# First attention's head loop: GpSimd negates the query factor, both state sums stand ahead of its power, three quantization passes move to slot 5, one C broadcast moves behind the attention products

## The reference, cut to what matters

```python
# layer 0, cross attention: 16 heads of 128, 4 batches of 256 queries and 256 keys
q = rmsnorm((hidden_states @ Wq).reshape(B, Sq, H, D), gq)
k = rmsnorm((encoder_hidden_states @ Wk).reshape(B, Skv, H, D), gk)
scores = einsum('bqhd,bkhd->bhqk', q, k) * scale
out = einsum('bhqk,bkhd->bqhd', softmax(scores), v) ... @ Wo
# layer 0, feed-forward: weights rounded in blocks of 32 to a tiny float format
q = round(x / scale) * scale, clipped to max_norm      # _q_w(w_gate), _q_w(w_up), _q_w(w_down)
# layer 3, state space block: 16 states, scanned over 256 steps for 4 batches and 256 channels
state = state * dA + (d * u)[..., None] * b[:, None, :]
y = einsum('bdn,bn->bd', state, c)                      # y is a sum over the 16 states
```

## Time and profile before

| | |
|---|---|
| median of 3 runs (lowest, highest) | 1078.1 us (1078.09, 1079.49) |
| profiled execution: its time, its span | 1078.1 us, 1076.6 us |
| PE busy | 878.0 us, 82% of the span |
| DVE busy | 764.5 us, 71% |
| ACT busy | 490.1 us, 46% |
| POOL busy | 332.1 us, 31% |

### The profile page before, as it was taken

The page is one execution under the profiler, slowest core; times in us unless marked ns, Lnnn a source line. Parts: engine busy times, 40 slices in busy tenths (PEclk is TensorE's granted clock), DMA queues, the critical chain, the costliest instruction groups (busy, mean ns, idle before and its releaser), DMA issues.

```text
span 1076.6 us, 12899 instructions
## 1 busy us (share of the span) xinstructions
PE 878.0 (82%) x4348; PEld 620.3 (58%) x4352; DVE 764.5 (71%) x1505; ACT 490.1 (46%) x855; POOL 332.1 (31%) x210
## 2 busy tenths in 40 slices
PE   5786988898989888865658988667687889999998
PEld 3355776666767666643335464454576776545656
DVE  5248799999998989889973856856889874353311
ACT  2484665565656555633321334443576664111111
POOL 2012244433333343425471000203465740510000
PEclk8899999999999999886677999885789999999999
DMA  3012000000000000000502000000000000300000
GB/s 120 16 40 93 16 15 15 24 20 15 15 15 15 15 17 1 5 0 1 190 0 79 1 0 1 1 1 1 1 1 2 1 1 1 125 0 1 10 10 20
DMA packets 12924, 24.25 MB, mean 23 GB/s; under 512 B 4280, under 2 KB 8656, under 8 KB 11728
## 3 DMA queue, kind: packets, MB, share of 16 engines
q1 hardware_dynamic: 12448, 20.53, 5.7%
q10 hardware_dynamic: 432, 3.15, 0.7%
HBM read 22.63 MB, written 1.05 MB: 22 GB/s over the span
## 4 chain that ended last, share of the span: by engine, by line
PE 29%; DVE 16%; issue 5%; ACT 4%; POOL 1%; ACTq 0%; DVEq 0%
PE PS L2088 12%; PE PS L2137 6%; PE PS L2191 3%; DVE mxf L1541 2%; DVE regD L1579 1%; PE PS L1992 1%; PE PS L1641 1%; PE PS L1968 1%; DVE regB L1579 1%; DVE regA L1291 1%; DVE mx_am L1242 1%; PE PS L2155 1%; PE PS L2006 1%; PE PS L2175 1%; PE PS L2176 1%
## 5 line engine op out<-in xcount | busy, mean ns | idle before, releaser
L476 POOL TENSOR_TENSOR y<-y,regB 128x1024 f32<-128x1024 f32 x32 | 76.3, 2389 | 162.7 <-DVE regB L1096 162.7
L450 POOL TENSOR_SCALAR veps<-mv 128x4 f32<-128x4 f32 x16 | 7.4, 463 | 273.7 <-DVE mv L977 273.7
L679 ACT ACTIVATE regA<-PS,nb,rq 128x256 f32<-128x256 f32 x128 | 71.4, 566 | 32.9 <-DVE regA L1057 31.7
L1057 DVE TENSOR_SCALAR_CACHE_REDUCE regA<-PS,nrq 128x256 bf16<-128x256 f32 x128 | 55.8, 473 | 31.7 <-PE PS L1716 30.0
L1747 PE MATMUL PS<-regA 128*128 128x256 f32 x256 | 69.6, 396 | 9.9 <-DVE X L1070 9.9
L2191 PE MATMUL PS<-regA 128*128 128x128 f32 x512 | 74.8, 294 | 3.4 <-ACT regA L931 3.3
L1085 DVE TENSOR_TENSOR_SCAN regB<-regB 128x1024 f32<-128x1024 f32 x32 | 72.8, 2279 | 0.1
L2191 PEld LDWEIGHTS PS<-regA 128*128 128x128 f32 x512 | 68.2, 207 | 7.1 <-ACT regA L931 6.0
L1738 PE MATMUL PS<-regA 128*128 128x256 f32 x256 | 67.4, 386 | 5.7 <-DVE qss L1044 5.6
L1716 PE MATMUL PS<-regA 128*128 128x256 f32 x256 | 66.8, 384 | 0.0
L1070 DVE SCALAR_TENSOR_TENSOR X<-PS,ls,X 128x256 f32<-128x256 f32 x128 | 55.4, 475 | 14.2 <-PE PS L1747 13.5
(11 more groups left out here) (270 smaller groups left out, 2140.9 us busy)
## 6 DMA issues: line engine op xcount, KB each, us to landing
regA<-in_W SPq DMA_DIRECT2D x16, 384.0 KB, 3.0
regB<-in_wg SPq DMA_DIRECT2D x2, 1024.0 KB, 6.5
regB<-in_wu SPq DMA_DIRECT2D x2, 1024.0 KB, 8.4
X<-in_x SPq DMA_DIRECT2D x1, 1024.0 KB, 7.6
regC<-in_wg ACTq DMA_DIRECT2D x1, 1024.0 KB, 4.7
regC<-in_wu ACTq DMA_DIRECT2D x1, 1024.0 KB, 7.4
regC<-in_wd ACTq DMA_DIRECT2D x1, 1024.0 KB, 10.4
regB<-in_wd SPq DMA_DIRECT2D x1, 1024.0 KB, 9.0
```

The source lines that it names most:

```text
L476: pool.tensor_tensor(halves(y3, i), halves(y3, i), halves(prod, i), ALU.add).then_inc(y_done, 1)
L679: act.activation(p0[i][:, q, :], bank(S_BANK + i)[:, q * S:(q + 1) * S], ACT.Exp, bias=nb0[:, i, q:q + 1], scale=rq[par][:, 2 * b + q:2 * ...
L1057: ins = dve.tensor_scalar(spill[:, i, q, :], bank(S_BANK + i)[:, q * S:(q + 1) * S], nrq[par][:, t:t + 1], None, ALU.mult, ALU.min, accum_ ...
```

## The change

Four edits, all in this loop. POOL computes `nrq` itself, with a product of `rq` and a tile of -1 right behind the power, and DVE only waits for it. On POOL the second y sum of a head goes ahead of the query power, behind the key power. DVE does its three quantization passes L1141 to L1143 at the end of slot 5 instead of slot 6. PE issues the broadcast of the second half of C (index 3) behind `heads` and `output` of slot b = 2 instead of ahead of them.

```diff
+        negone = sb("negone", [P, NT])
...
+            pool.memset(negone[:, :], -1.0).then_inc(const_set, 1)
...
-            pool.wait_ge(const_set, 4)
+            pool.wait_ge(const_set, 5)
...
             def query_scale(h, par):
                 pool.wait_ge(qss_done, h + 1)
                 pool.tensor_tensor(rq[par][:, :], qss[:, :], neghalf[:, 0:NT], ALU.pow).then_inc(rq_done, 1)
+                pool.wait_ge(rq_done, h + 1)
+                pool.tensor_tensor(nrq[par][:, :], rq[par][:, :], negone[:, :], ALU.mult).then_inc(nrq_done, 1)
...
                     scan_sum(n, 0)
                     key_scale(hp * 2 + (par + 1))
+                    scan_sum(n, 1)
                     query_scale(hp * 2 + (par + 1), 1 - par)
-                    scan_sum(n, 1)
                     (block_values if par else block_units)(hp)
...
-            def query_factor(h, par):
-                dve.wait_ge(rq_done, h + 1)
-                link(dve.tensor_scalar(nrq[par][:, :], rq[par][:, :], -1.0, None, ALU.mult))
...
-                elif s == 6:
+                elif s == 5:
                     dve.wait_ge(mxu_done, hp)
                     link(dve.tensor_scalar(mx_c.bitcast(I32), part.bitcast(I32), EXPO, None, ALU.bitwise_and))
                     link(dve.tensor_scalar(mx_c, mx_c, 1.0, 1.5 * 2.0 ** 22, ALU.max, ALU.mult))
                     link(dve.tensor_scalar(part, part, 6.0, -6.0, ALU.min, ALU.max))
...
-                            query_factor(h, par)
+                            dve.wait_ge(nrq_done, h + 1)
...
                         elif b == 2:
-                            broadcast_state(n, 3) if more else broadcast_state(n + 1, 1)
+                            if not more:
+                                broadcast_state(n + 1, 1)
...
                             output(hp * 8 + (s - 3), par if b >= 3 else 1 - par, (b + 1) % B)
+                        if b == 2 and more and not first:
+                            broadcast_state(n, 3)
```

More of the change, by code:

```diff
@@ L286, in build @@
         ksq_done, kss_done, rk_done, kn_done = sem("ksq_done"), sem("kss_done"), sem("rk_done"), sem("kn_done")
-        qsq_done, qss_done, rq_done = sem("qsq_done"), sem("qss_done"), sem("rq_done")
+        qsq_done, qss_done, rq_done, nrq_done = sem("qsq_done"), sem("qss_done"), sem("rq_done"), sem("nrq_done")
         s_mm, nb_done, exp_done, rl_done = sem("s_mm"), sem("nb_done"), sem("exp_done"), sem("rl_done")
@@ L511, in _ @@
             key_scale(H0 - 1)
+            scan_sum(H0 - 4, 1)
             query_scale(H0 - 1, 1)
-            scan_sum(H0 - 4, 1)
             for n in range(H0 - 3, H0 - 1):
@@ L605, in ln_out @@
                 last.then_inc(xnT_done, 1)
-            act.wait_ge(const_set, 4)
+            act.wait_ge(const_set, 5)
             for c in range(2):
@@ L1146, in quantize_weights @@
                     dve.tensor_tensor(part, part, mx_c, ALU.subtract).then_inc(mxr_done, 1)
-            LINKS = 2 * 2 + 7
+            LINKS = 2 + 7
             def pair(hp, first, last):
```

## The result

The changed kernel takes 1109.5 us (median of four runs, 1108.2 to 1111.1), the kernel before 1078.35 (four runs, 1078.1 to 1079.5): a ratio of 1.029, 95% interval 1.028 to 1.031. It is slower by 31.1 us; 1110, 31.9 us slower, was forecast. The profiled execution's span is 1107.0 us, against 1076.6.

What follows compares the result with a forecast made beforehand. PE and DVE were taken to bound the hardware loop in turns. Terms 2.90 - 1.88 + 0.1 + 1.8 + 2.4 = 5.3 us a pass, 31.9 over six passes, took 1078.1 to 1110 us; range 1094 to 1121.

Steps and rivals of the forecast that it cites:

- S: Start of transpose_k (L1701) on PE, a time mark in each half of a loop pass.
- A: Start of add_out on DVE in a slot b = 1, a time mark in each half of a loop pass.
- the halves: Two halves of a loop pass: the odd holds quantization passes L1141 to L1143, the even the block maxima mask L1136.
- odd half, A to S: the wait of L1142 and what follows: L1142 waits 2.05 us for POOL's first y sum, delaying score_max, L1709 and S: 2.90 us a pass later.
- odd half, S to A: PE sets it again: L1146's wait and nrq leave DVE, so 13.66 us becomes PE's 11.78: 1.88 us a pass back.
- negation on POOL: After the query power, POOL's negation can hold L1146 for its own length: 0.1 us, ends 0 and 1.5 a pass.
- even half: L1136 waits: L1136 comes 0.4 us after POOL's second y sum starts and waits for it: 1.8 us a pass.
- clock, fall ahead of L1709: PE idle about 5.75 us loses clock, slowing L1709 and the scores of slot 7: 2.4 us a pass.
- clock, second fall, even half: Rival: PE idle 2.8 us ahead of L1701 loses clock again, 2.4 us a pass more, 1124; chance 0.09.
- the 3.02 us of the earlier trace: A PE idle time before the change after which the clock did not fall, seen only once; L1738 took 1.10 us.
- DVE would need 13.66 - 2.05 - 1.08 = 10.5 us: S to A on DVE without L1146's wait and nrq; PE needs 11.78 us, so PE sets it.
- Powers: POOL's powers on 8 columns counted as not blocking DVE; rival that they exclude it: 1 us a pass more, 1116, chance 0.05.

Runs made afterwards that it cites:

- e3: Kernel before with one edit, POOL negating the query factor (nrq): 1077.4 us, ratio 1.000.
- e9: The changed kernel plus matmuls nobody reads, twelve ahead of L1709 in the odd half and four ahead of L1701 in the even half: 1094.2 us.
- e8: The changed kernel with quantization moved clear of the y sums, and L1141 and L1142 ahead of add_out of slot 5: 1054.8 us, ratio 0.979.
- e1: Kernel before with one edit, passes L1141 to L1143 at the end of slot 5: 1109.1 us, ratio 1.029.
- e2: Kernel before with one edit, the second y sum ahead of the query power: 1108.3 us, ratio 1.029.
- e10: The changed kernel with the second y sum back behind the query power and the negation: 1122.2 us, ratio 1.040.
- e5: The changed kernel plus matmuls nobody reads, eight ahead of L1709 in the odd half and four ahead of L1701 in the even half: 1101.5 us.
- e6: Kernel before with the second y sum ahead of the query power, plus four matmuls nobody reads ahead of L1701 in both halves: 1087.9 us.
- e11: The changed kernel with passes L1141 to L1143 back in slot 6: 1108.6 us, ratio 1.028.

## Why the prediction was right, point by point

The table sets each term beside what the changed kernel's rows give, in us a pass. S, A and the halves are those of the prediction; the clock term in the odd half is the mean distance from L1709 to S over six passes, 6.86 us, less the 5.04 us that the prediction's steps make without it.

| term | predicted | measured |
|---|---|---|
| odd half, A to S: the wait of L1142 and what follows | +2.90 | +2.84 |
| odd half, S to A: PE sets it again | -1.88 | -1.87 |
| negation on POOL | +0.1 | 0 (e3: +0.15 inside a wait that is gone here) |
| even half: L1136 waits | +1.8 | +1.83 |
| clock, fall ahead of L1709 | +2.4 | +1.82 (1.44 to 2.21) |
| clock, second fall, even half | a rival | +0.56 (1.68 in two of six passes) |
| sum | +5.3 | +5.18 from these terms; +5.22 by the passes' mean |

- **Passes in slot 5.** Right in mechanism and size: `score_max` of slot 6 comes 8.55 us after A (210.27 - 201.72), 4.31 later than before, of which 2.31 are the passes and 2.0 the wait. L1709 follows it by 2.08 us, S by 2.09 the maxima of slot 7.
- **Second y sum.** Right: L1146 at 1.22 us, S to A 11.79 us (230.71 - 218.92), L1136 at 2.02.
- **Clock.** Right in kind, wrong in size twice. The 2.2 to 2.9 us were worked out as if L1709 and the scores behind it both ran at the low clock, and 2.4 were put. L1709 did (3.5 to 3.8 us), but the scores (1.03 to 1.54) found the clock back or nearly so. The second fall, a rival held off by the 3.02 us of the earlier trace rows, happened in two passes. The two errors, -0.58 and +0.56, cancel, and that the sum came out within 0.1 us is luck to this extent. e9 confirms the total: its passes are 2.40 us shorter than those of the change.
- **A step that was wrong without effect.** "DVE would need 13.66 - 2.05 - 1.08 = 10.5 us": the 1.08 us of `nrq` are not on the way from S to A, as e3 showed. It did not reach the sum, since PE's 11.78 us was the larger in either case; taken alone it would have promised e3 a gain that is not there.
- **Powers.** They keep DVE from nothing here either: in the changed kernel the query power ran from 219.02 to 220.67, and L1145 started in it, at 219.86, and took its usual 1.22 us. The small product of the negation, 0.20 us alone, does meet DVE: 0.39 us in the odd half of the change, 1.13 in one place ahead of the loop, and in e8 0.96 to 0.98 in every odd half, where it ended just behind L1145 (205.94 and 205.88):

```profile
204.98 0.96 POOL L471 TENSOR_TENSOR nrq<-rq,negone 128x8 f32<-128x8 f32 x1
```

For these products and sums the trace agrees with the rule of the Trainium skill (SBUF — State Buffer, Who interferes with whom) that the prediction weighed; for the powers it still does not.

**Why two harmful edits cost no more than one.** The passes alone cost 31.0 us, the y sum alone 30.2, both together 31.1. Shown by rows: either edit alone brings one wait of 2 us into the stretch that delays S in the odd half (L1142 in e1, L1143 in e2) and a fall of the clock there. Together it is still one wait there, L1142: the passes are no longer in slot 6 when the second y sum comes, and DVE then stands idle for PE (2.29 us ahead of the scores' maxima at 216.83). The early y sum pays for its new wait in L1136 (+1.83) with the old one in L1146 (-1.87). The even half's fall of the clock came in five of six passes of e2 and in two of six of the change.

## What to carry to other kernels

Where two engines exclude each other, moving an instruction "into free time" is only half a plan: look at what the other engine starts there, because the short one that comes second pays all that is left of the long one (0.18 us became 2.02). Price an idle PE twice, once as time and once as what the fallen clock does to the work behind it; here the second was half of the loss, and a few unread matmuls show how much of a slowdown it is. An instruction that vanishes from the busier engine is worth something only if the engine that it holds up starts behind it: find the row that releases it.

## What the runs showed that was not expected

The length of an idle time alone did not decide whether PE's clock fell. In the loop it fell behind 2.03 us (e10, six of six passes), behind 2.27 us (e5, five of six) and behind 2.79 us (e2 five of six, the change two of six); it did not fall behind 3.02 us in the kernel before or behind 2.00 and 2.01 us in e1. A fall shortly before is no explanation by itself: those 2.00 and 2.01 us of e1 begin 12.4 and 12.6 us after the start of a slow L1709, the 2.03 us of e10 11.9 to 12.3 us after one. Nor is the place in the program. One idle time of 3.31 us, in the same place ahead of the loop in all thirteen kernels, left the clock high in eleven profiled executions, here that of the change, and brought it down in two, e10 and e6; first the change, then e10:

```profile
77.38 1.10 PE L1747 MATMUL PS<-regA 128*128 128x256 f32 x4 [3.31 <-DVE X L1070]
...
78.50 2.05 PE L1747 MATMUL PS<-regA 128*128 128x256 f32 x4 [3.31 <-DVE X L1070]
```

What decides it stays open, so for idle times of 2 to 3.3 us the fall can be priced but not forecast from these runs. Idle times of 3.4 us and more in the loop brought it every time (e2, e11, e1, the change, e10). One fall cost 1.4 to 2.8 us here.
